# Global attention on 128 + 64 doubled channels with paired pieces, and a patch stage that takes over the first statistics

## The chip, the cores and the metric

One core of a Trainium2 chip runs the whole program in one launch. The metric is the device time of that launch in microseconds (us). In the profile PE is the matrix engine's matmul side and PEld its weight loads, DVE the vector engine, ACT the scalar engine, POOL the GpSimd engine, SP the engine whose queue issues most DMAs; a q behind a name (SPq) is an engine's sequencer.

## What is computed

The input is 16 pictures of 3 x 96 x 96 and a text of 16 x 512 tokens of 192 channels, all fp32. Cut to what matters here:

```
h = patch_tokens(x)                    # layer norm over a picture, 1x1 convolution, 36 patches -> 192 channels
h = concat([h, txt], axis=1)           # 16 x 548 x 192
h = h + linear_attention(norm(h))      # 12 heads, random features
h = h + gated_attention(norm(h))       # 3 experts of 64 channels, below
h = h + talking_heads(norm(h))
h = h + experts(norm(h))
# gated_attention(x), for each picture:
gate = softmax(relu(x @ Wg1 + bg1) @ Wg2 + bg2); keep the best two of three
q, k = split(x @ Wqk + bqk)
for e in 0, 1, 2:
    v_e = x @ Wv[e] + bv[e];  q_0 is convolved along the tokens
    y_e = softmax(causal(q_e k_e' / 8)) v_e * gate_e
out = concat(y) @ Wp + bp
```

## The kernel before

The 548 tokens of a picture lie in five tiles of up to 110 rows in the resident tensor X. The program is a row of phases, and all engines meet at a barrier between two of them: patch_tokens, performer (the linear attention), gated_attention (called the global attention in the change's name), then talking heads and experts. Every engine's order is written out by hand; semaphores tie the engines together.

**patch_tokens.** Pictures come in six groups of up to three. DVE first builds the product of the 1x1 convolution and the projection (weff, nine instructions, lines 398 and 400, after waiting for the projection's DMA), then takes the statistics of all pictures (lines 405 to 419, with a matmul and a power on POOL in between), then scales and shifts each group (428, 430). PE transposes and multiplies, DVE adds the position term (place, 273) and POOL issues the DMAs of the finished rows into X (375). The text of pictures 0 to 7 is fetched meanwhile.

**performer.** DVE starts with stats and aggregate (763, 768, 772) of the ten tiles of pictures 0 and 1, POOL raises to the power -1/2 (692), DVE normalizes (norm, 780), PE transposes (1009), ACT copies (920), PE makes the keys (1021). SP issues the text of pictures 8 to 15, then the weights of gated_attention (lines 661 to 676), then the first spill of a transposed picture (681).

**gated_attention.** Pictures go in eight pairs. A pair is one *round* of STEP = 15 steps, five query tiles t times three kinds (expert 0 and 1 of one picture each with both experts, expert 2 of both pictures); step s of a round has t = s // 3, and its scores have (t + 1) * 110 keys. In step n PE does, in this order: turn(n-2) for the first of two halves (1684), a piece, turn(n-2) for the second, a piece, the late turn of the last key tile (1690), the output product of every third step (produce, 1699 and 1700), the scores of step n+1 (1735), the values of step n-3 (1754). DVE does the causal mask (1499), two maxima (1503), a copy of the values (1512 to 1515), norm and statistics of the next pairs' tiles, the gates (gates_first in step 9, gates_last in step 10), its share of the pieces' copies, then 1/sum and the gate's weight (1535, 1538), and adds the output product to X (1545). ACT copies the turned probabilities (PT, 1599), raises to the exponential (1606), each twice, with its share of the pieces' copies after each. POOL multiplies the probabilities (1370), convolves (1314 to 1322, steps 6 to 8 and 11 to 13) and makes the next rstd (1299). The five last-tile scores use all four score banks, so the scores of the steps 12 to 15 wait for both exponentials of the step before.

Beside a round PE makes the next pair's *pieces*, in the order of PLAN: X (transposed normalized tokens, xT, 1648), Q, K, E (1639; 275 tokens each, 128 outputs; E is expert 2's q and k), H (hidden layer of the gate, 1657), L (its logits, 1669) and V (1674). A piece's result goes to one of two PSUM banks in turn (MISC, by the piece's number m; the late turn and the output product have numbers too). `begin(m)` waits until piece m-2 was taken from the same bank:

```
def begin(m):
    if m >= 2:
        pe.wait_ge(taken[m % 2], m // 2)
    return MISC[m % 2]
```

ACT takes X, H (four instructions, 1567), Q (1572), K (1576) and V (1581); DVE takes E (1419, 1420) and L (1429, 1431). The 192 channels are two chunks of 96 partitions; the second has a 97th row of ones, which brings the biases into the matmuls. The last round has no pieces; a few idle matmuls (spare, 1783 and 1784) stand in for them.

Of the kernel before, what the change touches and what calls it, by code (L numbers as in the profile page):

```python
# [20 lines left out]
B = 16  # L21
# [132 lines left out]
def early_weights(k, pf_ctx, ga_ctx):  # L154
# [7 lines left out]
    ga.wqk = sb(ga_ctx, "ga_wqk", [C + 1, KC, 2 * D])  # L162
    ga.wv = sb(ga_ctx, "ga_wv", [C + 1, KC, D])
    ga.wg1 = sb(ga_ctx, "ga_wg1", [C + 1, KC, HID])
# [10 lines left out]
    pf.eps = sb(pf_ctx, "pf_eps", [128, 1])  # L175

# [20 lines left out]
def text(k, eng, A, images, landed):  # L197
    b0, b1 = images[0], images[-1] + 1
    txt = A["txt"][b0:b1].rearrange("b n d -> n b d")
    for r0, r1 in ((NPATCH, NPATCH + 64), (NPATCH + 64, R)):  # L200
        eng.dma_start(k.X[r0:r1, b0 * T:b1 * T:T, :], txt[r0 - NPATCH:r1 - NPATCH]).then_inc(landed, 16)
    for t in range(1, T):
        n0 = t * R - NPATCH
        eng.dma_start(k.X[0:rows(t), b0 * T + t:b1 * T:T, :], txt[n0:n0 + rows(t)]).then_inc(landed, 16)


def patch_tokens(k, A):
# [5 lines left out]
    with ExitStack() as ctx:  # L213
# [37 lines left out]
        centred, scaled, normed = sem("centred"), sem("scaled"), sem("normed")  # L251
        turned, xT_in, prod, added, placed = sem("turned"), sem("xT_in"), sem("prod"), sem("added"), sem("placed")
# [8 lines left out]
        with nc.Block() as block:  # L261
# [80 lines left out]
            def _(pool):  # L342
# [29 lines left out]
                for b in range(B):  # L372
                    g, j = b // G3, b % G3
                    pool.wait_ge(added, g + 1)
                    pool.dma_start(X[0:NPATCH, b * T, :], y[j * NPATCH:(j + 1) * NPATCH, g, :]).then_inc(placed, 16)
                pool.wait_ge(placed, 16 * B)

            @block.vector
            def _(dve):
# [11 lines left out]
                dve.wait_ge(proj_in, 32)  # L391
                for c in range(CH):
                    for o in range(CH):
# [17 lines left out]
                dve.tensor_tensor(mv[:, :, 1], mv[:, :, 1], sq[:], ALU.add).then_inc(stats, 1)  # L411
                dve.wait_ge(averaged, 1)
# [13 lines left out]
                for g in range(NG3):  # L426
# [131 lines left out]
def performer(k, A):  # L558
# [13 lines left out]
    with ExitStack() as ctx:  # L572
# [3 lines left out]
        st = sb("st", [R, NT, 6])  # L576
        mv = sb("mv", [R, NT, 2])
        ve = sb("ve", [R, B, T])
        rstd = sb("rstd", [R, B, T])
# [29 lines left out]
        stat, aggr, var, powed, xn_in = (sem(n) for n in ("stat", "aggr", "var", "powed", "xn_in"))  # L609
# [7 lines left out]
        text_in, ga_in, warmed = (sem(n) for n in ("text_in", "ga_in", "warmed"))  # L617
        ga = k.ga
        NGA = 16 * (4 * 2 + 2 * E0 + 2 + 4 + 3 + 2)
# [23 lines left out]
        with nc.Block() as block:  # L643
            @block.sync
            def _(sp):
# [13 lines left out]
                text(k, sp, A, range(B // 2, B), text_in)  # L659
                for src, n, dst in ((0, 128, 0), (D, 128, 128), (128, 64, 256), (D + 128, 64, 320)):  # L660
                    sp.dma_start(ga.wqk[0:C, :, dst:dst + n], chunked(A["L0_ffn_Wqk"])[:, :, src:src + n]).then_inc(ga_in, 16)
                    sp.dma_start(ga.wqk[C:C + 1, KC - 1, dst:dst + n], row(A["L0_ffn_bqk"])[:, src:src + n]).then_inc(ga_in, 16)
                for e in range(E0):
                    sp.dma_start(ga.wv[0:C, :, e * HD0:(e + 1) * HD0], chunked(A["L0_ffn_Wv"][e])).then_inc(ga_in, 16)
                    sp.dma_start(ga.wv[C:C + 1, KC - 1, e * HD0:(e + 1) * HD0], row(A["L0_ffn_bv"][e])).then_inc(ga_in, 16)
                sp.dma_start(ga.wg1[0:C], chunked(A["L0_ffn_Wg1"])).then_inc(ga_in, 16)
                sp.dma_start(ga.wg1[C:C + 1, KC - 1, :], row(A["L0_ffn_bg1"])).then_inc(ga_in, 16)
# [20 lines left out]
            def _(pool):  # L688
                pool.memset(low[:], 3.0e38).then_inc(filled, 1)
                pool.wait_ge(filled, 1)  # L690
                pool.wait_ge(var, 1)
                pool.tensor_tensor(rstd[:, 0, :], ve[:, 0, :], k.mhalf[0:R, 0:T], ALU.pow).then_inc(powed, 1)
                pool.wait_ge(powed, 1)
                pool.memset(e[:, :, :, 2 * M:PW], 1.0).then_inc(filled, 1)
                pool.wait_ge(filled, 2)
                pool.memset(v1[:, :, :, W34:VW], 1.0).then_inc(filled, 1)
# [3 lines left out]
                for b in range(B + 2):  # L700
                    if b == 4:
                        pool.wait_ge(ga_in, NGA)
                        for c, s in ((C + 1, slice(128, 256)), (C + 1, slice(320, 384))):
                            pool.tensor_scalar(ga.wqk[0:c, KC - 1, s], ga.wqk[0:c, KC - 1, s], HD0 ** -0.5, None, ALU.mult)
                            pool.tensor_scalar(ga.wqk[0:C, 0, s], ga.wqk[0:C, 0, s], HD0 ** -0.5, None, ALU.mult)
# [52 lines left out]
            def _(dve):  # L758
# [43 lines left out]
                for u in range(T):  # L802
                    stats(u)
                for u in range(T):
                    aggregate(u)
                for u in range(T, 12):
                    stats(u)
                for u in range(T, 10):
                    aggregate(u)
                norm(0)  # L810
                norm(1)
                dve.wait_ge(filled, 4)
# [1997 lines left out]
```

## Time and profile before

| | |
|---|---|
| median of three runs | 4689.63 us (4688.78 to 4690.82) |
| the profiled execution, its own time | 4690.51 us |
| its span, first to last instruction | 4688.7 us |
| patch_tokens | 0 to 62.1 us |
| performer | 62.1 to 736.5 us |
| gated_attention | 736.5 to about 1303 us |
| talking heads and experts | to the end |

Times in rows count from the span's start. "A:B" rows sum a stretch; a timeline row merges neighbouring instructions of one kind and begins with its start and its length. An fp32 matmul of the program is two records of the profile, and matmul ends are modelled, so the distance from one start to the next is the safer reading. In brackets stands the idle time before an instruction and what ended it.

### The profile page before, as it was taken

The numbers are of one execution on the slowest core, as the hardware profiler recorded it, in microseconds if no ns is written. First come the engines' busy times: TensorE is split into PE (matmuls) and PEld (weight loads), VectorE is DVE, ScalarE is ACT, GpSimd is POOL, SyncE is SP. The second block draws the span as 40 slices with busy tenths as digits, with TensorE's granted clock in tenths as the row PEclk, the third lists the DMA queues.
The fourth block names the chain that finished last, engine by engine and source line by source line (L and its number), as shares of the span: only waits on it lengthen the run. The fifth ranks groups of instructions, "written<-read, shape, count | busy, mean of one in ns | idle before, by whom it ended". The sixth has DMA issues, their size and how long they took to land. (4 is left out here: it accounts for less than half of the span.)

```text
span 4688.7 us, 141401 instructions
## 1 busy us (share of the span) xinstructions
PE 4554.5 (97%) x58206; PEld 3744.1 (80%) x58206; DVE 2549.3 (54%) x7440; ACT 2183.1 (47%) x5035; POOL 1671.0 (36%) x2777
## 2 busy tenths in 40 slices
PE   6999998999889999999999999999999999999998
PEld 4666665776678888888888888888888888899998
DVE  5667886666555555455555555555555544442333
ACT  3443443555545554554455455445545544212443
POOL 1103335777633333333333333333333333001555
PEclk8999999999999999999999999999999999999999
DMA  4112110000000000000000000000000000232333
GB/s 109 23 30 48 38 31 7 1 2 1 1 14 2 13 13 2 20 13 13 3 13 13 2 13 13 7 8 13 13 2 13 13 3 17 74 90 66 65 65 56
DMA packets 122476, 110.77 MB, mean 24 GB/s; under 512 B 63975, under 2 KB 110396, under 8 KB 121844
## 3 DMA queue, kind: packets, MB, share of 16 engines
q1 hardware_dynamic: 94447, 66.34, 6.1%
q0 software_dynamic: 16768, 23.59, 2.9%
q10 hardware_dynamic: 10628, 11.80, 1.1%
q8 instruction: 472, 7.73, 0.7%
q14 instruction: 161, 1.31, 0.1%
HBM read 59.76 MB, written 41.48 MB: 22 GB/s over the span
## 5 line engine op out<-in xcount | busy, mean ns | idle before, releaser
L1937 POOL TENSOR_TENSOR th_qg<-th_qT,w_th_th 128x180 f32<-128x180 f32 x1760 | 846.3, 503 | 1617.1 <-PE PS L2231 1607.5
L2231 PE MATMUL PS<-th_kT,th_qg 64*125 64x274 f32 x10560 | 1420.5, 400 | 0.0
L2130 ACT ACTIVATE th_P<-PS 110x600 f32<-110x600 f32 x880 | 647.0, 735 | 1119.1 <-PE PS L2218 1119.1
L2048 DVE TENSOR_REDUCE th_nmx<-PS 125x1 f32<-125x548 f32 x880 | 641.0, 728 | 902.8 <-PE PS L2231 902.8
L2218 PEld LDWEIGHTS PS<-th_mixn,th_P 61*110 61x110 f32 x17600 | 985.8, 173 | 96.0 <-issue 20.2
L2231 PEld LDWEIGHTS PS<-th_kT,th_qg 64*125 64x125 f32 x10560 | 947.5, 184 | 136.9 <-issue 0.2
L2218 PE MATMUL PS<-th_mixn,th_P 61*110 61x60 f32 x17600 | 980.2, 254 | 3.5 <-ACT th_P L2130 1.8
L2140 ACT ACTIVATE th_P<-PS,th_nb 125x548 f32<-125x548 f32 x880 | 621.0, 706 | 106.9 <-DVE th_nb L2051 106.9
L1370 POOL TENSOR_SCALAR ga_P<-ga_P,ga_rw 110x110 f32<-110x110 f32 (+4 forms) x240 | 264.9, 1115 | 160.3 <-DVE ga_rw L1538 159.5
L2051 DVE TENSOR_SCALAR th_nb<-th_nmx,w_th_b 125x1 f32<-125x1 f32 x880 | 240.1, 273 | 32.2
L2256 PEld LDWEIGHTS PS<-th_P,th_v 110*32 110x32 f32 x11520 | 229.7, 110 | 28.6 <-issue 27.5
L2256 PE MATMUL PS<-th_P,th_v 110*32 110x90 f32 (+1 forms) x11520 | 250.2, 244 | 2.1 <-issue 1.2
L2065 DVE TENSOR_SCALAR th_mixn<-w_th_mix,th_rs 125x60 f32<-125x60 f32 x880 | 225.0, 256 | 31.8
L2455 POOL DMA_INDIRECT ex_cx<-ex_tokens,ex_token_of x77 | 77.0, 1000 | 343.1 <-DVE ex_b L2629 250.7
L1021 PE MATMUL PS<-w_pf_wK,pf_xT 64*110 64x456 f32 x960 | 196.1, 555 | 1.4 <-ACT pf_xT L920 1.4
L1599 ACT ACTIVATE ga_PT<-PS 110x440 f32<-110x440 f32 (+3 forms) x240 | 102.3, 426 | 199.2 <-PE PS L1684 196.8
L2387 ACT ACTIVATE ez_h<-PS,ex_cb 128x128 f32<-128x128 f32 x462 | 127.5, 375 | 133.3 <-PE PS L2715 133.3
L2468 POOL DMA_INDIRECT out_h<-ex_cy,ex_token_of x77 | 132.9, 1726 | 136.5 <-DMA out_h<-ex_cy,ex_token_of 120.5
L2400 ACT ACTIVATE ez_h<-PS,ex_bz 128x550 f32<-128x550 f32 x96 | 68.9, 719 | 241.2 <-PE PS L2654 241.2
L2140 ACT ACTIVATION_READ_ACCUMULATOR th_P<-PS,th_nb 125x1 f32 x880 | 178.1, 202 | 0.0
L2715 PE MATMUL PS<-ex_cxT,ex_wz 64*128 64x128 f32 x2772 | 175.5, 278 | 0.3 <-ACT ex_cxT L2418 0.3
L2715 PEld LDWEIGHTS PS<-ex_cxT,ex_wz 64*128 64x128 f32 x2772 | 160.7, 188 | 13.4 <-issue 12.8
(364 smaller groups left out, 6407.3 us busy)
## 6 DMA issues: line engine op xcount, KB each, us to landing
pf_xT<-pf_spill SPq DMA_DIRECT2D x32, 412.5 KB, 5.4
ex_tokens<-th_xn SPq DMA_DIRECT2D x124, 82.5 KB
pf_spill<-pf_xT SPq DMA_DIRECT2D x16, 412.5 KB, 3.7
ex_turned<-th_rT SPq DMA_DIRECT2D x16, 412.5 KB, 3.1
ex_x<-ex_turned SPq DMA_DIRECT2D x32, 206.2 KB, 4.4
out_h<-X SPq DMA_DIRECT2D x16, 330.0 KB
ex_w<-in_L_ffn_W ACTq DMA_DIRECT2D x18, 288.0 KB
ex_w<-in_L_ffn_W ACTq DMA_DIRECT2D x8, 576.0 KB
```

Of the source, the lines that this page charges most:

```text
L1021: ins = pe.matmul(PS[0:R, p + a, 0:HM + D], xT[half, slot(u), c, cols(u)], wK[half, c, :], start=c == 0, stop=c == NC - 1)
L1370: pool.tensor_scalar(P[:, n % 4, u, 0:keys(t)], P[:, n % 4, u, 0:keys(t)], rw[:, n % 4, u:u + 1], None, ALU.mult).then_inc(scaled, 1)
L1937: ins = pool.tensor_tensor(qg[:, m % SB, :, 64 * s:64 * s + HQ].rearrange("p c (h n) -> p c h n", n=QH), qT[:, im % 2, :, at + s * QH:at + ...
L2048: dve.tensor_reduce(nmx[:, p:p + 1], PS[0:MR, bank:bank + 2, 0:HK], AX.XY, ALU.max, negate=True) \
L2051: dve.tensor_scalar(nb[:, p:p + 1], nmx[:, p:p + 1], b1[:, 0:1], b1[:, 0:1], ALU.subtract, ALU.add) \
L2065: dve.tensor_scalar(mixn[:, p], mix[:], rs[:, p:p + 1], None, ALU.mult).then_inc(scaled, 1)
L2130: act.activation(P2[:, :, :, at * QT:(at + 1) * QT].rearrange("p t h (s n) -> p s (t h) n", s=2), PS[0:R, MB:MB + 2, 0:VO].rearrange("p s ...
L2140: act.activation(P[:, p, 0:N].rearrange("p (a n) -> p a n", a=2), PS[0:MR, bank:bank + 2, 0:HK], ACT.Exp, bias=nb[:, p:p + 1], accum_out=r ...
L2218: ins = pe.matmul(PS[0:R, MB + s, t * HQ:(t + 1) * HQ], P[a, p, t * R:(t + 1) * R], mixn[a, p], start=True, stop=True)
L2231: ins = pe.matmul(PS[0:MR, bank + a, 0:HK], qg[s, p, c, 0:MR], kT[s, im % 2, c, :], start=c == 0, stop=c == NC - 1)
L2256: ins = pe.matmul(PS[32 * j:32 * j + 32, bank, c * nq:(c + 1) * nq], v[:, b % 2, t].rearrange("p h d -> p (h d)")[:, at:at + 32], P2[:, t, ...
L2715: ins = pe.matmul(PS[:, 2 + 2 * (j % 2) + a, i * SL:(i + 1) * SL], cw[s, j % 2, c, i, :], cxT[s, j % 2, c, :], start=c == 0, stop=c == NC - 1)
```

## The change

- The tokens' 192 channels are 128 in one chunk and 64 in another, and these 64 are written twice, on partitions 0 to 63 and 64 to 127; so are their weights. norm has a second instruction for the copy.
- Q, K, E and V pieces are made in *groups* of two, in both banks: first both matmuls over 128 channels, then the two over 64 channels, each on its own half of the rows. `give` takes both banks first. PLAN is new.
- The biases leave the matmuls: ACT adds them when it copies H, Q and K, DVE when it copies E, and V moves from ACT to DVE as an addition.
- The weights come in 44 DMAs and not 25.
- In patch_tokens weff is built in three parts behind steps of the statistics, and the statistics of pictures 0 and 1 of performer are taken there (token_stats), with the first power on POOL.

```
+def token_stats(k, dve, tiles):
+    for u in tiles:
+        dve.bn_stats(pf.st[:, u, :], k.X[:, u, :]).then_inc(pf.stat, 1)
+    for u in tiles:
+        dve.wait_ge(pf.stat, u + 1)
+        dve.bn_aggr(pf.mv[:, u, :], pf.st[:, u, :]).then_inc(pf.aggr, 1)
...
+                    if b == B - 2:
+                        pool.wait_ge(pf.var, 1)
+                        pool.tensor_tensor(pf.rstd[:, 0, :], pf.ve[:, 0, :], k.mhalf[0:R, 0:T], ALU.pow).then_inc(pf.powed, 1)
...
                 dve.tensor_tensor(mv[:, :, 1], mv[:, :, 1], sq[:], ALU.add).then_inc(stats, 1)
+                weigh(0)
                 dve.wait_ge(averaged, 1)
...
+                weigh(1)
                 dve.wait_ge(powed, 1)
...
+                weigh(2)
                 dve.wait_ge(w_in, 16 * (2 + G3))
...
+                dve.wait_ge(text_in, 16 * (T + 1))
+                dve.wait_ge(placed_first, 16 * G3)
+                token_stats(k, dve, range(0, T))
                 place(dve, NG3 - 2)
+                token_stats(k, dve, range(T, 2 * T))
                 place(dve, NG3 - 1)
...
-        PLAN = ((("X", 0, 0),), (("X", 0, 1),), (("X", 0, 2),), (("X", 1, 0),), (("X", 1, 1), ("Q", 0, 0)),
-                (("X", 1, 2), ("Q", 0, 1)), (("H", 0, 0), ("K", 0, 0)), (("K", 0, 1),), (("L", 0, 0), ("E", 0, 0)),
-                (("E", 0, 1), ("Q", 1, 0)), (("Q", 1, 1), ("K", 1, 0)), (("K", 1, 1), ("E", 1, 0)), (("E", 1, 1), ("V", 0, 0)),
-                (("V", 0, 1), ("V", 0, 2)), (("V", 1, 0), ("V", 1, 1), ("V", 1, 2)))
+        PLAN = ((one("X", 0, 0),), (one("X", 0, 1),), (one("X", 0, 2),), (one("X", 1, 0), both("Q", 0)), (one("X", 1, 1),),
+                (one("X", 1, 2),), (one("H"), both("K", 0)), (both("Q", 1),), (one("L"), both("K", 1)), (both("E", 0),),
+                (both("E", 1),), (both("V", 0),), (both("V", 1),), ((("V", 0, 2), ("V", 1, 2)),), ())
...
+                        dve.tensor_scalar(xn[:, m % 4, D:2 * 128], X[:, b * T + t, 128:D], mv[:, b, t, 0:1],
+                                          rstd[:, p, b % 2, t:t + 1], ALU.subtract, ALU.mult).then_inc(xn_in, 1)
...
+                    if kind == "V":
+                        dve.wait_ge(given[m % 2], m // 2 + 1)
...
+                        dve.tensor_tensor(v[:, p % 2, i, 2 * j:2 * j + tiles, :],
+                                          PS[0:R, bank, 0:tiles * D].rearrange("p (t d) -> p t d", t=tiles),
+                                          bv[:].unsqueeze(1).broadcast_to([R, tiles, D]), ALU.add).then_inc(taken[m % 2], 1)
...
+                def give(n, group):
+                    kind, i, j = group[0]
                     p = n // STEP + 1
+                    ms = [number[n, piece] for piece in group]
+                    banks = [begin(m) for m in ms]
...
+                        w = slice("QKE".index(kind) * 128, ("QKE".index(kind) + 1) * 128)
+                        for g in range(2):
+                            pe.matmul(PS[:, banks[g], 0:HALF], wqk[:, 0, w], xT[:, i, 0, g * HALF:(g + 1) * HALF], start=True, stop=False)
+                        for g in range(2):
+                            half = slice(g * PC, (g + 1) * PC)
+                            pe.matmul(PS[:, banks[g], 0:HALF], wqk[half, 1, w], xT[half, i, 1, g * HALF:(g + 1) * HALF],
+                                      start=False, stop=True).then_inc(given[ms[g] % 2], 1)
```

## Rows read from the trace of the kernel before

**Rows 1.** Busy time of two phases: stretch, length, each engine's busy us (instructions), PEclk, DMA.

```profile
0.00:62.08 62.08, 29.68 (x154) 26.73 (x154) 31.41 (x65) 16.07 (x21) 12.59 (x37) 0.82 0.55 124
736.47:1303.00 566.53, 531.79 (x4168) 381.99 (x4168) 360.77 (x1256) 301.70 (x952) 389.59 (x346) 0.99 0.01 3
```

**Rows 2.** One steady round, mask to mask: steps 0-8, 9, 10, 11-14 (PE, PEld, DVE, ACT, POOL).

```profile
970.65:1003.53 32.88, 31.17 (x267) 21.33 (x265) 23.07 (x87) 19.66 (x71) 19.32 (x21) 1.00 0.01 1
1003.53:1009.28 5.75, 5.40 (x38) 3.63 (x37) 5.35 (x19) 2.88 (x8) 5.70 (x5) 1.00 0.01 3
1009.28:1014.36 5.08, 4.66 (x32) 3.10 (x32) 4.11 (x17) 2.35 (x8) 3.04 (x3) 1.00 0.00 0
1014.36:1037.21 22.85, 22.54 (x191) 18.06 (x188) 12.58 (x38) 12.52 (x32) 19.93 (x14) 1.00 0.01 1
sum 66.56, PE 63.77 PEld 46.12 DVE 45.11 ACT 37.42 POOL 47.99; mean PE 15.94 PEld 11.53 DVE 11.28 ACT 9.35 POOL 12.00
```

**Rows 3.** Steps 0 to 13 of a round with pieces, and of the last without.

```profile
970.65:1030.38 59.73, 56.95 (x452) 40.09 (x452) 42.35 (x151) 33.40 (x109) 42.05 (x38) 1.00 0.01 2
1235.78:1291.69 55.91, 46.27 (x394) 32.73 (x396) 28.73 (x95) 26.36 (x86) 30.17 (x29) 1.00 0.01 1
```

**Rows 4.** Timeline of PE: a K piece, four V tiles' matmuls, a pair of scores.

```profile
886.90 1.11 PE L1639 MATMUL PS<-ga_xT,w_ga_wqk 96*128 96x275 f32 x4
887.85 0.54 PE L1684 MATMUL PS<-ident,ga_P 110*110 110x110 f32 x4
...
892.23 1.47 PE L1674 MATMUL PS<-w_ga_wv,ga_xT 96*110 96x192 f32 x8
893.54 0.54 PE L1684 MATMUL PS<-ident,ga_P 110*110 110x110 f32 x4
...
935.48 0.62 PE L1735 MATMUL PS<-ga_k,ga_qc 64*110 64x440 f32 x1
935.93 0.53 PE L1735 MATMUL PS<-ga_k,ga_qc 64*110 64x440 f32 x1
```

**Rows 5.** Timeline of PEld in performer: loads for two 64-row matmuls.

```profile
153.59 0.18 PEld L1021 LDWEIGHTS PS<-w_pf_wK,pf_xT 64*110 64x110 f32 x2 [0.20 <-issue]
153.98 0.18 PEld L1021 LDWEIGHTS PS<-w_pf_wK,pf_xT 64*110 64x110 f32 x2 [0.20 <-issue]
```

**Rows 6.** Timeline of ACT: H taken in step 6, a PT copy in step 12.

```profile
993.00 1.60 ACT L1567 ACTIVATE ga_g<-PS 32x275 f32<-32x275 f32 x4 [0.16 <-PE PS L1657]
...
1021.55 0.54 ACT L1599 ACTIVATE ga_PT<-PS 110x440 f32<-110x440 f32 x1
```

**Rows 7.** Timeline of DVE: step 10's gates, the output's addition, E's second copy.

```profile
1012.82 0.19 DVE L1470 TENSOR_TENSOR ga_g<-ga_ge,ga_kept 110x30 f32<-110x30 f32 x1 [0.69 <-ACT ga_ge L1614]
...
1013.89 0.55 DVE L1545 TENSOR_TENSOR X<-PS,X 110x384 f32<-110x384 f32 x1
...
1074.63 0.45 DVE L1420 COPY ga_k<-PS 64x273 f32<-64x273 f32 x1
```

**Rows 8.** Timeline of POOL: first scaling of step 11, and the power of step 13.

```profile
1018.84 2.74 POOL L1370 TENSOR_SCALAR ga_P<-ga_P,ga_rw 110x440 f32<-110x440 f32 x2 [2.03 <-DVE ga_rw L1538]
...
1034.34 1.97 POOL L1299 TENSOR_TENSOR ga_rstd<-ga_ve,mhalf 110x10 f32<-110x10 f32 x1
```

**Rows 9.** Timeline of DVE in patch_tokens and at performer's start.

```profile
18.28 0.42 DVE L398 TENSOR_SCALAR tk_weff<-tk_projT,tk_cw 128x384 f32<-128x384 f32 x1 [12.42 <-DMA tk_projT<-in_tok_proj_wT]
...
23.56 5.62 DVE L405 BATCH_NORM_STATS2 tk_st<-tk_img 108x6 f32<-108x384 f32 x12
...
62.12 1.40 DVE L763 BATCH_NORM_STATS2 pf_st<-X 110x6 f32<-110x192 f32 x5 [4.37 <-PEq L2747]
...
66.35 1.59 DVE L780 TENSOR_SCALAR pf_xn<-X,pf_mv,pf_rstd 110x384 f32<-110x384 f32 x2
```

**Rows 10.** Timeline of SP: the first spill behind the weights; ACT: picture 3's copies.

```profile
87.27 27.19 SPq L681 DMA_DIRECT2D pf_spill<-pf_xT  x3
...
113.53 0.79 ACT L920 ACTIVATE pf_xT<-PS 128x330 f32<-128x330 f32 x2
```

More of the change, by code:

```diff
@@ L1210, in scores, with both, one, groups @@
             return flat[0:R, at:at + keys(t)]
-        PLAN = ((("X", 0, 0),), (("X", 0, 1),), (("X", 0, 2),), (("X", 1, 0),), (("X", 1, 1), ("Q", 0, 0)),
[3 rows of a table removed]
+        def both(kind, i):
+            return (kind, i, 0), (kind, i, 1)
+        def one(kind, i=0, j=0):
+            return ((kind, i, j),)
+        PLAN = ((one("X", 0, 0),), (one("X", 0, 1),), (one("X", 0, 2),), (one("X", 1, 0), both("Q", 0)), (one("X", 1, 1),),
+                (one("X", 1, 2),), (one("H"), both("K", 0)), (both("Q", 1),), (one("L"), both("K", 1)), (both("E", 0),),
+                (both("E", 1),), (both("V", 0),), (both("V", 1),), ((("V", 0, 2), ("V", 1, 2)),), ())
         TURN, GIVE, TAKE, OUT = 2, 3, 4, 5
+        def groups(n):
+            return PLAN[n % STEP] if n // STEP + 1 < PAIRS else ()
         def pieces(n):
-            return PLAN[n % STEP] if n // STEP + 1 < PAIRS else ()
+            return tuple(piece for group in groups(n) for piece in group)
         def late(n):
@@ L1627, in begin @@
                     return MISC[m % 2]
-                def give(n, piece):
-                    kind, i, j = piece
+                def give(n, group):
+                    kind, i, j = group[0]
                     p = n // STEP + 1
-                    m = number[n, piece]
-                    bank = begin(m)
-                    at = slice(j * HALF, (j + 1) * HALF)
-                    tiles = range(2 * j, min(2 * j + 2, T))
-                    def half(wc, rows_out):
-                        for c in range(KC):
-                            ins = pe.matmul(PS[0:rows_out, bank, 0:HALF], wc(c), xT[0:kin(c), i, c, at], start=c == 0, stop=c == KC - 1)
-                        return ins
+                    ms = [number[n, piece] for piece in group]
+                    banks = [begin(m) for m in ms]
+                    bank = banks[0]
@@ L1676, in give @@
-                    ins.then_inc(given[m % 2], 1)
+                            for c in range(2):
+                                x0 = ((t - 2 * j) * 2 + c) * R
+                                ins = pe.transpose(PS[:, bank, x0:x0 + R], xn[:, q % 4, c * 128:(c + 1) * 128], ident[0:R, 0:R])
+                        ins.then_inc(given[ms[0] % 2], 1)
+                        return
+                    for ii in range(2) if kind == "H" or j == 2 else (i,):
+                        for jj in range(3):
+                            wait_taken(pe, (p, ("X", ii, jj)))
@@ L1763, in _ @@
                 for n in range(FIRST, END):
-                    ps = pieces(n)
+                    gs = groups(n)
                     for u in range(2):
@@ L1771, in _ @@
                             stream(1)
-                        if u < len(ps):
-                            give(n, ps[u])
-                    for piece in ps[2:]:
-                        give(n, piece)
+                        if u < len(gs):
+                            give(n, gs[u])
                     if late(n):
```

202 lines of the change are left out of this document (108 added, 94 removed).

## The prediction

> **What bounds the kernel now.** I read first the busy time by phase. The changed matmuls are all in gated_attention, 566.5 us long, with PE busy for 531.8 of them; the patch phase is 62.1 us long and keeps no engine busy for much over half of that [rows 1]. Next the windows of one steady round, cut at the mask of each step. A round takes 66.56 us and PE is busy for 63.77: by this view alone PE is the bound. But the reader is to see two windows beside it: in step 9 DVE is busy for 5.35 of 5.75 us, and in steps 11 to 14 POOL for 19.93 of 22.85 [rows 2]. Then the comparison that tells what PE work is worth. The last round makes no pieces: PE has 10.7 us less to do in fourteen steps, DVE 13.6 less, and these steps take 55.91 us instead of 59.73 [rows 3]. So even without any piece a round gains only 3.8 us; behind PE stands a chain score, mask, exponential, turn, PT copy, next score that is almost as long. Whether the change wins depends on what its waits do to that chain, more than on PE's sum.
>
> **What PE saves.** A Q, K or E piece occupies PE for 887.85 - 886.90 = 0.95 us: four records of 275 columns, 0.2375 each. Eight V records of 192 columns take 893.54 - 892.23 = 1.31, or 0.164 each [rows 4]. Two 64-row matmuls that run together take the time of one: in performer 0.39 us from one pair of records with 456 columns to the next [rows 5], in the scores 0.45 with 440 columns, where full-rate columns would take 0.38 [rows 4]. The score pair enters and leaves row halves, the performer's pair stays in them; I book 0.09 us a record pair, between 0 and 0.09. A group of Q, K or E is then 4 x 0.2375 + 2 x (0.2375 + 0.09) = 1.60 instead of 1.90, a V group of four tiles 1.31 + 4 x 0.164 + 0.18 = 2.14 instead of 2.62, the group of two last tiles 1.16 instead of 1.31. Six groups save 1.8, the V groups 1.1: 2.9 us a round, up to 4.4 if switching is free. The X transposes have as many records as before and stay as they are.
>
> The Trainium skill, "TensorEngine Tiling (Array Packing)", section Theoretical Speedup, gives up to 2x where a dimension is at most 64; by that the saving would be the 4.4 us. The same page, Key Properties, says that changing the tiling mode drains the engine, and there the score pair's extra 0.09 agrees; by it the saving is the 2.9.
>
> **What waits.** A group takes both banks at its start, so it waits until the piece right before it was taken, where before PE wrote one bank while the other was emptied. And PLAN moves work forward: until step 8 there were five Q, K or E pieces (4.75 us), now four groups (6.4): +1.6. I go through a round.
>
> Steps 0 to 8: the group of Q behind X waits for ACT's copy of X, 0.5. The group of K in step 6 waits for all four copies of H, 1.60 us on ACT [rows 6], of which the turn between covers 0.24: +1.4. In step 7 the output product waits for the first Q copy, +0.3; in step 8 K waits for DVE to take L, +0.5. PE idles 1.7 us in these steps now [rows 2], and the shorter steps 4 and 5 give back about 1.3 of such waits. Sum +1.6 + 0.5 + 1.4 + 0.3 + 0.5 - 1.3 = +3.0. DVE's second norm instruction (64 of 192 columns, 0.2 us, two a step) disappears in DVE's waits except in step 0.
>
> Step 9: DVE takes two E pieces, not one, after gates_first. One is two copies of 0.45 [rows 7], so +0.9, of which 0.4 us was idle [rows 2]: +0.5.
>
> Step 10: this is the worst place. Both E pieces are taken by DVE behind gates_last, which itself waits for ACT's exponential of step 10 [rows 7]. The output product of the same step needs the bank of the first, and the scores of step 11 are queued behind it on PE. From the mask at 1009.28 the gates' wait ends at 1012.82, the gates at +4.3, the first E at +5.2, the output product (eight records of 192 columns, 1.31) at +6.5, the next mask after 0.9 of scores and hand-over, +7.5 less 0.2 because ACT has nothing to take before: 7.3 instead of 5.08, +2.2.
>
> Steps 11 and 12: the whole V group of 2.14 stands between the two turns, where a piece of 0.95 stood. The second PT copy and the second exponential queue behind the second turn (0.54 [rows 6] and 0.9 with the hand-over), and the scores of a last tile wait for that exponential: +1.2 each, +2.4. That V is on DVE as 0.55 [rows 7] adds nothing there, DVE is idle for 10.3 us of these four steps [rows 2].
>
> Steps 13 and 14: PE has 1.16 and nothing instead of four V groups' worth, yet little comes back. POOL works without a gap from the scaling at 1018.84 to the end of the power at 1036.31 [rows 8], DVE's norm of step 14 waits for that power, and the next mask is behind it on DVE. I give back 0.4 and add 0.4 for the norm's second instructions: 0.
>
> The sum is 3.0 + 0.5 + 2.2 + 2.4 = +8.1 us a round. Seven rounds carry pieces: +57. Lower bound of a round: none of the new waits shows, and it gains what taking all pieces away gains, -3.8 [rows 3]. Upper bound: no wait is given back, +1.3, and the gates' step costs 1 us more: +10.5. Before round 0 the pieces stand alone; there PE and the copies alternate, the V groups save 1.5, E waits for its copies: -2, between -5 and +5.
>
> **The patch stage.** DVE waits 12.42 us for the projection, builds weff until 23.56 and only then starts the statistics [rows 9]. The pictures' DMAs were issued at the very start; they have landed by 23.56, since nothing waits there, and I take 16.5, between 13 and 18 (1.7 MB at the phase's rate of 124 GB/s and some more [rows 1]). Statistics at 16.5: -7.1. weff's three parts are 1.7 us each; two fill the waits for the mean and the power (+1.0 and +0.3 beyond them), the third comes whole before the next work, +1.7: -4.0 in all, between -1 and -6. Behind it token_stats costs DVE 2 x 2.0 us, mostly while PE multiplies, and POOL's power stands ahead of the last DMA: +0.8. In performer the statistics go, from 62.12 to the norm at 66.35: -4.2, and -0.3 as that norm runs alone [rows 9]. Sum -8, between -3 and -11. The removed ones-row memset and the smaller memset of v1 lie beside other work: 0.
>
> Nineteen DMAs more on SP, 0.3 to 0.6 us each, push the first spill from 87.27 to 93 - 99; its buffer is overwritten by picture 3's copies at 113.53 [rows 10]. Hidden; were it not, each us late would be a us.
>
> **Sum.** 4690.5 (the profiled run's own time, 0.9 above the median) + 57 - 2 - 8 = 4737.5; against the median 4737.
>
> **The rivals.**
> 1. The waits overlap. PE is one step ahead of DVE at many places, and a late piece may be caught up before its reader. Then a round costs +2 to +4: 4690 + 21 - 10 = 4701, up to 4715. For it: PE's idle 1.7 us in steps 0 to 8 [rows 2]. Against: the chain of step 10 has no slack, since DVE itself is the late one.
> 2. Faster: PE is the bound as its busy share says, and the copies keep up with the groups. Place: the bank waits in steps 6, 8 and 10; from the point where they sum to less than PE's 2.9 us the round shortens. Seven rounds by -2.9 and -10: 4660, at the bound of -3.8 4653. Against: H's 1.60 on ACT and gates_last ahead of E on DVE stand in the program's order.
> 3. The array packing does nothing: halves run one after the other. Against: the performer's pairs run together [rows 5]. A round costs another 3 to 4 us: 4760.
> 4. No change: gain and waits cancel (a round +1): 4687 to 4698.
>
> The Trainium skill, same page, section PSUM Bottleneck, says that tiling speeds up the multiplication and not the emptying of PSUM; and Gotcha 1 says that two row tiles can't use one bank at once. That is the rule by which a group must take both banks, as forecast. No row here shows two halves in one bank.
>
> **How the numbers follow.** Forecast (a round +5 to +10, 4716 to 4757) 0.57; rival 1 0.16; rival 4 0.08; rival 2 0.11; rival 3 or longer 0.08. The range 4699 to 4762 holds the forecast, rival 1 and most of rival 3. About 0.2% (9 us) is what a measurement tells from no change: faster by more 0.12, within 0.09, slower 0.79. The forecast's own range is 4716 to 4757.
>
> **What would show it.** In the profile after: rounds of 71 to 76 us between step-0 masks; step 10 at 7.3 us with the output product released by DVE's E copy; PE waiting about 1.4 us behind H in step 6; steps 11 and 12 about 1.2 longer with the scores released by the exponential; performer's first matmul near 60 us and not 68; the spill still ahead of its reader. It would be wrong if step 10 stays near 5 us, or if the group's wait in step 6 is hidden.

## The result, and the profile after

The changed kernel takes 4828.43 us in the median of four runs (4813.28 to 4831.44), against 4689.73 for the kernel before on the same chip: a ratio of 1.029, 95% interval 1.027 to 1.031. It is slower, as forecast, but by 139 us and not by 47; the time lies outside the range of 4699 to 4762. The profiled execution is the fastest of the four, 4813.28 us with a span of 4811.5, so I first account for its 122.8 us of span, and then for the 15 to 18 us between it and the others.

Windows of the changed kernel: the patch phase, gated_attention whole, and its start up to the first mask [rows 1].

```profile
0.00:58.86 58.86, 29.38 (x154) 26.23 (x154) 34.77 (x87) 16.06 (x21) 13.92 (x38) 0.88 0.59 131
...
731.09:1425.80 694.71, 571.45 (x4150) 383.25 (x4152) 409.04 (x1382) 295.37 (x904) 387.60 (x345) 0.90 0.01 2
...
731.09:787.14 56.05, 40.85 (x158) 24.42 (x158) 23.52 (x98) 8.51 (x20) 21.08 (x29) 0.70 0.06 12
```

Gated_attention starts 5.4 us earlier (731.09, before 736.47) and is 128 us longer [rows 1]. PE is busy for 40 us more, although it has less to multiply, and the column behind the engines, TensorE's granted clock, is 0.90 where it was 0.99. The seven rounds with pieces, from the first mask to that of the last round, went from 459.3 to 571.0 us (787.14 to 1358.15), so +111.7; the stretch ahead of them from 40.0 to 56.05, +16.0; the rest is +0.4.

Windows of one steady round of the changed kernel: steps 0 to 8, 9, 10, 11, 12 to 14 [rows 2].

```profile
1195.09:1235.54 40.45, 36.92 (x269) 24.97 (x270) 24.88 (x92) 22.19 (x74) 22.27 (x23) 0.87 0.01 1
1235.54:1242.05 6.51, 5.33 (x43) 3.21 (x44) 6.03 (x21) 2.79 (x9) 2.67 (x3) 1.00 0.00 1
1242.05:1251.97 9.92, 6.62 (x25) 3.81 (x25) 6.39 (x21) 1.89 (x6) 5.49 (x4) 0.73 0.00 0
1251.97:1258.99 7.02, 5.79 (x46) 4.28 (x48) 3.41 (x10) 2.29 (x6) 0.85 (x1) 0.90 0.01 2
1258.99:1278.41 19.42, 15.46 (x145) 11.41 (x146) 10.96 (x30) 8.19 (x20) 16.65 (x12) 0.97 0.00 1
sum 83.32, PE 70.11 PEld 47.68 DVE 51.66 ACT 37.34 POOL 47.94; mean PE 14.02 PEld 9.54 DVE 10.33 ACT 7.47 POOL 9.59
```

This is what the prediction did not have: a clock column below 1.00 in four of the five windows, where before it is 1.00 in all four. PE now idles for 13.2 us of a round (83.32 - 70.11); it idled for 2.8. Step 10 shows how the two hang together. First the output product and the scores of step 10 in the kernel before, then the timeline of PE and of DVE in step 10 of the changed kernel, whose mask is at 1242.05 [rows 7]:

```profile
1011.42 0.58 PE L1699 MATMUL PS<-w_ga_wpa,ga_c 128*110 128x192 f32 x2 [0.42 <-ACT ga_q L1572]
...
1012.91 0.99 PE L1735 MATMUL PS<-ga_k,ga_q 64*110 64x440 f32 x4
1013.84 0.79 PE L1754 MATMUL PS<-ga_PT,ga_v 110*64 110x110 f32 x12
```

```profile
1243.49 0.49 PE L1742 MATMUL PS<-ident,ga_P 110*110 110x110 f32 x3
1247.29 0.98 PE L1757 MATMUL PS<-w_ga_wpa,ga_c 128*110 128x192 f32 x2 [3.30 <-DVE ga_k L1462]
...
1250.12 1.81 PE L1793 MATMUL PS<-ga_k,ga_q 64*110 64x440 f32 x4
1251.86 0.45 PE L1812 MATMUL PS<-ga_PT,ga_v 110*64 110x110 f32 x2
```

```profile
1245.30 0.19 DVE L1521 TENSOR_TENSOR ga_g<-ga_ge,ga_kept 110x30 f32<-110x30 f32 x1 [0.39 <-ACT ga_ge L1661]
...
1246.21 0.50 DVE L1460 TENSOR_SCALAR ga_q<-PS,w_ga_bqk 64x275 f32<-64x275 f32 x1
1246.73 0.51 DVE L1462 TENSOR_SCALAR ga_k<-PS,w_ga_bqk 64x275 f32<-64x275 f32 x1
```

The gates' wait ends 3.25 us behind the mask (forecast 3.54) and the first E copy 5.2 (forecast 5.2). Up to here the forecast holds. But PE sat still for 3.3 us, and the output product then takes 2.83 us (1247.29 to 1250.12) where it took 1.49 before (1011.42 to 1012.91; the forecast had 1.31), and the scores 1.74 instead of 0.93. The granted clock of this step is 0.73: it stood at half in part of it. Step 10 takes 9.92 us, not 7.3.

PE's waits in the same round of the changed kernel: total us, times, the longest.

```profile
PE PS L1793 <- ACT ga_P L1653: 3.8, 3, 1.3
PE PS L1757 <- DVE ga_k L1462: 3.3, 1, 3.3
PE PS L1730 <- issue: 3.2, 3, 1.8
PE PS L1742 <- ACT ga_PT L1646: 1.3, 3, 0.7
```

The first three were forecast: scores behind the second exponential, the output product behind E, the groups behind H, L and E (a group waits for two banks, which the view puts down to "issue"; in this round 1.80 behind H, 0.22 behind L and 1.18 behind E). The turns' wait for a PT copy is not new, the kernel before has 1.3 us of it in a round too.

### The profile page after: what moved, and what is told of

It reads as the page before. It is cut to its first block and busy times, and to the rows that moved or that the text cites. A ratio compares the mean times of both kernels' runs of the same rounds, so it can differ in the third digit from the quotient of the medians.

```text
span 4811.5 us, 141359 instructions
## 1 busy us (share of the span) xinstructions
PE 4597.0 (96%) x58206; PEld 3747.3 (78%) x58206; DVE 2597.7 (54%) x7568; ACT 2176.7 (45%) x4987; POOL 1663.7 (35%) x2776
```

## The experiments

All times are medians; the kernel before had 4689 to 4691 us beside each. My theory from the trace of the changed kernel was A: the groups' waits are the cause, and the clock doubles their price. The rival B: what the layout brought (copies with a bias, V on DVE, the second norm instruction, the 64-row matmuls) costs the time even without groups. In the expectations C says that idle time costs once as a wait and once as the half clock behind it, W that the waits alone cost; the others are told where they stand.

**The front alone.** The kernel before with token_stats, weigh() and performer's shorter start; gated_attention and its loads as before.

> Only the front of the change: the pictures' statistics ahead of weff's parts, token_stats in the patch stage, the smaller memset; gated_attention, its weights and its loads are the kernel before's. In the trace of the changed kernel gated_attention starts 5.4 us earlier than before, although 19 more loads were issued. Theory A (the front is a gain of its own that the rounds then lose many times over): 4682 to 4685. Rival: the gain ahead of performer is given back at the border to gated_attention: 4689 to 4691.

4683.24 (4680.76 to 4685.16, ten runs), ratio 0.998, interval 0.9972 to 0.9991: a small gain and the only version here that is faster than the kernel before. Windows of the kernel before, of about 200 and 272 of PE's matmuls in performer, and of the same matmuls in the front-only kernel, followed by its start of gated_attention:

```profile
376.80:401.80 25.00, 19.64 (x202) 11.61 (x202) 16.30 (x33) 8.72 (x17) 11.36 (x33) 1.00 0.16 36
706.30:736.47 30.17, 22.31 (x272) 15.18 (x272) 22.93 (x49) 8.39 (x13) 7.57 (x19) 0.94 0.00 1
```

```profile
367.00:394.10 27.10, 21.43 (x203) 12.50 (x202) 16.36 (x33) 8.73 (x17) 11.49 (x33) 0.94 0.15 32
698.40:731.47 33.07, 26.96 (x272) 18.79 (x272) 23.10 (x49) 8.46 (x14) 7.59 (x19) 0.76 0.01 1
731.47:768.52 37.05, 34.12 (x157) 24.28 (x158) 18.64 (x81) 10.36 (x26) 23.07 (x30) 0.89 0.09 18
```

Performer's first matmul starts at 58.57 instead of 68.02, 9.5 us earlier, and up to 367 the same matmuls stay 9.8 us ahead: the edit gains more than the forecast's 8. Then the clock falls to half at two other places than before, and these two windows give back 2.1 and 2.9 us; gated_attention starts 5.0 us earlier. There the clock happens to be better (0.89 instead of 0.83) and 3.0 come back: the first mask is at 768.52 instead of 776.48, 8.0 earlier. Waits of which nothing was changed have moved against the clock. The -8 of the forecast comes out at the first mask, but by three errors that cancel (+1.8, -4.8, +3.0): that is luck.

**Pieces one at a time.** The changed kernel with the order of before and groups of one.

```
-                (one("X", 1, 2),), (one("H"), both("K", 0)), (both("Q", 1),), ...
+                (one("X", 1, 2), one("Q", 0, 1)), (one("H"), one("K", 0, 0)), (one("K", 0, 1),), ...
```

> The changed kernel with the pieces made one at a time by the order of the kernel before; layout 128 + 64, biases in the copies, V on DVE and the two norm instructions stay as changed. Theory A (the groups' waits for two banks and what follows from them are the whole loss; PE's sum is then that of before, 0.95 us a piece): 4680 to 4695. Theory B (the new copies, V on DVE, the second norm instruction or the second matmul on 64 rows cost the time by themselves): above 4750. Halfway means both.

4797.95. Theory A was half wrong: without any group 115 of the 145 us over the front-only kernel are still there (in the profiled executions the seven rounds sum to 557.7 us, against 459.8 in the front-only kernel and 571.0 in the changed one). Three things show in its trace. First, a piece: the timeline of PE in the version with V on ACT (below), at the full clock; the same rows stand in both.

```profile
1201.69 0.65 PE L1729 MATMUL PS<-ga_xT,w_ga_wqk 128*128 128x275 f32 x2
1202.26 0.73 PE L1732 MATMUL PS<-ga_xT,w_ga_wqk 64*128 64x275 f32 x2
1202.92 0.59 PE L1741 MATMUL PS<-ident,ga_P 110*110 110x110 f32 x4
```

A piece alone takes 1.23 us (1201.69 to 1202.92) against 0.95 [rows 4]: going into the row half and out again costs 0.28, and nothing runs beside it. My theory had 0.95. The Trainium skill, "TensorEngine Tiling (Array Packing)", Key Properties, says that changing the tiling mode drains the engine; this row agrees. Second, PE waits for DVE in step 14:

```profile
1267.64 0.90 PE L1724 MATMUL PS<-w_ga_wv,ga_xT 64*110 64x192 f32 x4
1270.74 0.58 PE L1718 MATMUL PS<-w_ga_wv,ga_xT 128*110 128x192 f32 x2 [2.21 <-DVE ga_v L1470]
```

Third, in step 9, which DVE bounds, one comparison of 110 x 10 elements takes 1.41 us. The same line has 0.174 in the kernel before. DVE, then POOL in that kernel:

```profile
1233.02 0.19 DVE L1505 TENSOR_TENSOR ga_gd<-ga_g,ga_gm 110x30 f32<-110x30 f32 x1
1233.24 1.41 DVE L1506 TENSOR_TENSOR ga_kept<-ga_g,ga_m 110x10 f32<-110x10 f32 x1
```

```profile
1233.29 1.33 POOL L1364 TENSOR_TENSOR ga_qc<-ga_qc,ga_side 64x548 f32<-64x548 f32 x1
```

It ends 0.03 us behind POOL's addition, which fits a wait for it. Its line has a median of 1.41 us over the eight rounds.

**V back on ACT**, V's bias left out of the computation, with single pieces, and with the groups.

> The kernel with single pieces (4798), V taken by ACT as before instead of DVE; V's bias is left out of the computation. Step 14 took 9.6 to 10.5 us there instead of 6.8, with PE waiting 2.6 us for DVE's add of V, which stands behind the norm and so behind POOL's power. Theory D (V on DVE is what the layout costs in step 14, and through the clock in steps 0 and 1): steps 14, 0 and 1 go back to 14.1 us from about 19.8, 4750 to 4762. Rival (the norm's second instruction and the wider X copies are late there): above 4785.

> The changed kernel with V taken by ACT, V's bias left out of the computation. My prediction's step (V on DVE adds nothing, DVE is idle for 10.3 us of these four steps): 4824 to 4832. Theory D, from the single pieces, where V on ACT gave back 52 us: at least half of that here, 4776 to 4802.

With single pieces 4745.91: 52 us less, theory D holds. Step 14 goes from 9.6 - 10.2 us to 6.73. With the groups 4827.85, no change: there my prediction's step stands, V on DVE adds nothing, because the groups put V into steps 11 to 13, away from the norm. So the 115 us of the single version are not all in the changed kernel; the two have different diseases. The single version also gives the cleanest sight of the clock. Two of its rounds, with the same instructions:

```profile
1153.67:1225.16 71.49, 67.72 (x520) 44.37 (x518) 50.16 (x169) 39.34 (x119) 48.00 (x41) 1.00 0.01 1
936.03:1010.69 74.66, 70.94 (x520) 46.18 (x518) 50.35 (x168) 39.46 (x119) 48.00 (x41) 0.95 0.01 1
```

71.49 at the full clock, 74.66 where step 10 fell into the half clock. And at the full clock PE has 67.7 us of work where it had 63.8 [rows 2]: twelve pieces of Q, K and E at 0.28 more are 3.4 of these 3.9 us.

**The second norm instruction** left out as well; the doubled channels are zero.

> Single pieces with V on ACT (4746, rounds of 71.49 us at the full clock against 66.59 with the old layout), and the norm's second instruction left out too, so that the doubled channels are zero. Theory N (DVE's second instruction, 0.31 us, two a step, costs the 0.9 in step 0 and shifts the compare in step 9 under POOL's addition, where it took 1.41 us instead of 0.17): a round 0.9 to 2.5 shorter, 4728 to 4740. Rival (X copies on 128 partitions and the H copies with a bias): 4744 to 4747.

4748.16: no gain. Its full-clock rounds take 71.3 us, 0.2 less, and the comparison in step 9 still takes 1.41. Theory N falls: the instruction is hidden, as forecast, and the meeting with POOL comes from elsewhere.

**Matmuls that nobody reads, to keep PE busy while it waits.** The first try wrote them to VB in steps 6, 10, 11, 12 and 14, the second to the free score banks in step 10, the third is the second with the right number:

```
+                            pe.wait_ge(exped, 2 * n)
+                            for _ in range(count):
+                                pe.matmul(PS[:, 2 * ((n + 1) % 2), 0:2 * D], ident[0:C, :], wqk[0:C, 0, :], start=True, stop=True)
```

> The changed kernel with matmuls of 384 columns that nobody reads where PE waits: 5 ahead of K in step 6, 3 ahead of E in step 10, 9 ahead of the output product of step 10, 3 each ahead of the scores in steps 11, 12 and 14. No other work is changed and no wait is shortened. Theory A1 (the granted clock falls to half after these waits, for 20.4 of the 83.3 us of a steady round, and the work then takes twice its time): a round 6 to 9 us shorter, 4765 to 4785. Rival A2 (the waits alone are the price, the clock only goes along): 4828, or some us more for the fillers that outlast their wait.

> The changed kernel with 12 matmuls of 384 columns that nobody reads in step 10 alone, 3 ahead of the E group and 9 ahead of the output product, written to the score banks of the next step, which are free by a wait that the scores of the next step have anyway. PE idled 1.3 and 3.3 us at these places. Theory C (the idle time costs once as a wait and once more as the half clock behind it: output product 2.83 us instead of 1.49, scores 1.74 instead of 0.92): step 10 falls from 9.9 to about 7.7 us, a round by 2.2, 4828 to 4805 to 4815. Theory W (waits only, the half clock would be there anyway or costs nothing): no change, or some us more.

> As the run with twelve such matmuls in step 10, with as many as fit the idle time: one took 0.645 us there (two records), not 0.33, so nine outlasted their wait by 2.4 us. Here 1 ahead of the E group and 5 ahead of the output product. Theory C: the output product then takes 1.4 us and the scores 0.93 at the full clock; step 10 takes 8.1 to 8.3 us instead of 9.92, and 4828 becomes 4812 to 4818, less if the clock falls elsewhere instead. Theory W: 4828 or above.

4854.7, 4832.64, 4800.2. The first two were badly built: one filler takes 0.645 us, not the 0.33 that I had used, so they outlasted the waits, and those of the first waited ahead of step 10's group for DVE's copy of VB (the bank of the values), which held up the turn, ACT's exponential and the gates (step 10: 17.0 us). Only the third tests the theory. Windows of its steps 10 and 11:

```profile
1227.87:1235.64 7.77, 7.71 (x33) 4.38 (x32) 6.52 (x22) 1.89 (x6) 3.64 (x3) 1.00 0.01 2
1235.64:1242.02 6.38, 5.14 (x46) 3.76 (x44) 3.42 (x10) 2.29 (x6) 2.55 (x3) 1.00 0.00 0
```

Its output product and scores, timeline of PE:

```profile
1233.28 0.58 PE L1757 MATMUL PS<-w_ga_wpa,ga_c 128*110 128x192 f32 x2
...
1234.77 0.99 PE L1793 MATMUL PS<-ga_k,ga_q 64*110 64x440 f32 x4
```

Step 10 takes 7.77 instead of 9.92 us, step 11 6.38 instead of 7.02, with six matmuls more to do: 2.8 us a round, 20 of the 28 in seven rounds (the profiled seven rounds sum to 552.3 us, 18.7 less). The output product is back at 1.49 us (1233.28 to 1234.77). No wait was taken away; only what PE did in it changed. (The other 8 lie where the half clock falls in the rest, the last round above all: two of the four runs have 4791 and 4793, two 4808 and 4812; the profiled one, 4812, has 77.71 us in the last round.)

> The kernel with single pieces (4798), with 5 such matmuls ahead of Q in step 10 (PE idle 2.0 us there) and 7 ahead of the last V piece of step 14 (PE idle 2.6 us there). After both places its trace shows the half clock for 6.8 to 10.2 us, and step 10 takes 8.3 to 9.0 instead of 5.08, step 0 5.3 to 5.5 instead of 3.03. Theory C: steps 10, 11, 0 and 1 give back about 2.2 + 1 + 2.2 + 1 us a round, 4750 to 4765. Theory W: 4798 or above.

4777.86, 20 us less instead of 33 to 48. Every steady round is at the full clock and step 10 takes 6.17 instead of 8.3 - 9.0, but seven fillers in step 14 were again too many (11.2 us instead of about 9.9).

> The changed kernel, with such matmuls in PE's waits ahead of round 0 alone (1 to 3 ahead of each group of Q, H, K, L, E and V, 17 in all, in VB, which nothing reads yet). The stretch from the phase's start to the first mask took 56.0 us instead of 40.0, with the clock at half for most of 748 to 779, and a group of Q, K or E 3.4 us instead of 1.7. Theory C: 5 groups at 1.7 us less: 46 to 49 us for the stretch, 4818 to 4821. Theory W (the copies set the pace, PE's speed doesn't matter there): 54 us or more, 4826 or above.

4818.1. The stretch ahead of the first mask:

```profile
729.40:777.62 48.22, 43.18 (x190) 24.40 (x190) 24.99 (x99) 8.50 (x20) 21.10 (x29) 0.93 0.07 14
```

48.2 us instead of 56.05, at a granted clock of 0.93 instead of 0.70. Half of the +16 was the clock.

**The order on DVE.** E ahead of gates_last in step 10; then E ahead of the gates in steps 9 and 10; then the same in the front-only kernel.

```
+                    for piece in pieces(n):
+                        take(n, piece)
                     if s == 10:
                         gates_last(p + 1)
-                    for piece in pieces(n):
-                        take(n, piece)
```

> The changed kernel, DVE takes the two E pieces of step 10 ahead of gates_last instead of behind it. E was given at 1243.49 and taken from 1246.21 in the trace. Theory A: the output product comes 2.7 us earlier, 19 us in seven rounds; with the half clock that follows this wait gone too, up to 5.2 a round: 4792 to 4809. Rival (the gates, later by the two copies, hold the scaling and so the turns up): 4825 or above.

> The changed kernel with the same swap in steps 9 and 10. With step 10 alone it took 4784. Theory S: E0 leaves its banks 1.6 us earlier, so E1 is given and the turn behind it comes earlier, a round 1 to 2 us less: 4770 to 4778. Rival: step 9 is DVE's own chain, 4782 to 4788.

> The front of the change alone (4683), with DVE taking the piece of step 9 ahead of gates_first and that of step 10 ahead of gates_last. PE idles 0.5 us in step 10 for the bank of the E piece of step 9. Theory S (the bank comes free 1.6 us earlier): 0.5 us a round less, 4677 to 4681. Rival (DVE itself is the chain in step 9, busy 5.35 of 5.75 us, so its order changes nothing, and the second exponential comes later): 4683 to 4688.

The first gives 4784.28, 44 us less: the best single edit to the changed kernel, at the step that I had named the worst. It was expected to give 19 to 36, and the rounds give 32 of that (539.3 us in the profiled seven, against 571.0); the rest of the 44 is the last round, which takes 61.04 us here and probably some 77 in most runs of the changed kernel (below). One of its rounds has the full clock up to the end of step 14. Its steps 0 to 8, 9, 10, 11, 12 to 14:

```profile
1095.42:1132.58 37.16, 32.14 (x266) 21.38 (x268) 24.81 (x92) 21.59 (x73) 22.32 (x23) 1.00 0.01 2
1132.58:1139.10 6.52, 5.33 (x43) 3.21 (x44) 6.04 (x21) 2.80 (x9) 2.69 (x3) 1.00 0.00 0
1139.10:1145.83 6.73, 5.46 (x39) 3.43 (x37) 6.26 (x21) 1.89 (x6) 3.16 (x3) 1.00 0.00 1
1145.83:1151.42 5.59, 4.35 (x33) 2.95 (x32) 3.41 (x11) 2.40 (x6) 3.19 (x3) 1.00 0.00 0
1151.42:1170.87 19.45, 15.46 (x145) 11.42 (x146) 10.98 (x31) 8.20 (x20) 16.68 (x12) 0.98 0.01 1
sum 75.45, PE 62.74 PEld 42.39 DVE 51.49 ACT 36.89 POOL 48.05; mean PE 12.55 PEld 8.48 DVE 10.30 ACT 7.38 POOL 9.61
```

75.45 us, still 8.9 above 66.56. The second swap loses instead of gaining: 4802.83, and 4698.35 in the front-only kernel (ratio 1.0016, interval 1.0007 to 1.0025; its rival was right, and by more than it said). The rounds carry it: 556.8 us in seven, 17.5 more than with the first swap. In the front-only kernel step 9 grew from 5.76 to 6.39 us, and again POOL's timeline tells why. DVE, then POOL:

```profile
1074.62 1.21 DVE L1473 TENSOR_TENSOR ga_gd<-ga_g,ga_gm 110x30 f32<-110x30 f32 x1
```

```profile
1074.45 1.33 POOL L1342 TENSOR_TENSOR ga_qc<-ga_qc,ga_side 64x548 f32<-64x548 f32 x1
```

The swap pushed a 0.19 us subtraction under POOL's addition, and it took 1.21. From the second round on steps 10 and 11 together then take 11.3 to 12.9 us instead of 9.7, with the half clock in step 10.

**K0 ahead of H**, in step 4, so that it doesn't wait for H's copies.

> The changed kernel with the group of K0 in step 4 behind X instead of in step 6 behind H. PE waited 1.8 us for the copies of H in step 6, and the half clock followed for 3.4 us. My prediction's step (K behind H costs 1.4 a round): step 6 falls from 6.9 to 4.9 us and step 4 grows by about 1: a round 1 to 2.5 shorter, 4810 to 4822. Rival: step 4 pays all of it: 4826 to 4832.

4845.52, 17 us more: a miss. Step 6 fell to 4.96 us as expected and step 7 from 6.1 to 4.4, but step 4 rose from 3.2 to 6.5, step 9 by 1.1, step 10 by 1.6. In step 9 the gates' first product, 0.19 us elsewhere, took 1.30, under the same addition of POOL.

**The last round, and all together.**

> The changed kernel with one unread matmul of 384 columns in each of the first four steps of the last round. Theory L (its timed runs, 4828, entered the last round at the half clock and stayed there, 77 us instead of 57; its profiled run, 4813, didn't): all runs at 4811 to 4818. Rival (the 15 us lie elsewhere): 4826 to 4832.

> The swap in steps 9 and 10, the unread matmuls ahead of round 0 and in the last round, two more ahead of K in step 6 and one ahead of the scores in steps 11, 12 and 14: the changed kernel as near the full clock as fillers that fit its waits bring it. Theory C (half of the loss is the clock, half the waits and switches, which stay): half clock for under 60 us of the phase, 4735 to 4755, still above 4690. Rival 1 (the clock was nearly all): 4690 or below. Rival 2 (the fillers only trade waits): above 4765.

> The swap in step 10 alone (4784), with the unread matmuls ahead of round 0, in the first four steps of the last round, two ahead of K in step 6 and one ahead of the scores in steps 12 and 14. Theory C: rounds of 75.5 to 76.5 us, as the one of that kernel without a half clock, and 8 us less ahead of round 0: 4755 to 4766, so at the full clock the change would still be 70 us slower. Rival (the clock is all that is left): below 4730. Rival (fillers only trade waits): 4775 or above.

4813.59 (4812.88 to 4819.16), 4774.19 and 4764.59. The first bears on the 15 to 18 us between the profiled run of the changed kernel and its others, of which no trace was kept. Windows of the last round, of the changed kernel, of the one with fillers ahead of round 0, and of the one with groups and V on ACT:

```profile
1358.15:1415.67 57.52, 47.88 (x394) 33.74 (x396) 28.74 (x94) 26.35 (x86) 30.98 (x29) 0.97 0.01 1
```

```profile
1347.92:1422.84 74.92, 65.29 (x394) 45.71 (x396) 29.20 (x95) 26.32 (x86) 30.73 (x29) 0.69 0.00 1
```

```profile
1358.35:1436.03 77.68, 68.05 (x394) 47.22 (x396) 29.20 (x95) 26.31 (x86) 30.72 (x29) 0.65 0.00 1
```

The same 394 records take 57.5 or 77.7 us, and the seven rounds ahead of them sum to 571.0 and 571.1 us in the first and the third kernel: the 20 us between their profiled runs (4813 and 4833) are the last round. Where the clock falls to half at its border, within 2 us to either side, it stays there for 54.6 us in the third kernel and for 47.8 in the second. With the four unread matmuls the round takes 62.95 us at 0.92, so they keep about three quarters of it away. The last run brings theory C's 4755 to 4766: three of its seven rounds take 75.44 to 75.47 us, at a granted clock of 0.98 to 1.00. With most of the clock restored and with the best order found the change is still 74 us slower than before: 62.6 of that are the seven rounds and 8.4 the last, which takes 64.31 us at 0.89. The second run, both swaps with fillers, lies on the side of its rival 2; the half clock still fell in step 10 of every round.

## Why the prediction was right or wrong

The direction was right, and so were the new waits of the rounds and the steps in which they stand; the size was a third, because the forecast had no term for the clock and almost none for the stretch ahead of round 0. One round, by step; the third column is put together from the rows of the full-clock round (steps 0 to 9 and 12 to 14, whose order the swap leaves as it is) and of the third filler run (10 and 11):

| steps | before | forecast | at the full clock | measured |
|---|---|---|---|---|
| 0 to 8 | 32.88 | +3.0 | 37.16, +4.3 | 40.45, +7.6 |
| 9 | 5.75 | +0.5 | 6.52, +0.8 | 6.51, +0.8 |
| 10 | 5.08 | +2.2 | 7.77, +2.7 | 9.92, +4.8 |
| 11 | 4.64 | +1.2 | 6.38, +1.7 | 7.02, +2.4 |
| 12 to 14 | 18.21 | +1.2 | 19.45, +1.2 | 19.42, +1.2 |
| sum | 66.56 | +8.1 | 77.28, +10.7 | 83.32, +16.8 |

Timeline of PE in the third filler run: one group at the full clock, which ends at 1223.97.

```profile
1222.27 1.11 PE L1730 MATMUL PS<-ga_xT,w_ga_wqk 128*128 128x275 f32 x4
1223.31 0.73 PE L1733 MATMUL PS<-ga_xT,w_ga_wqk 64*128 64x275 f32 x4
```

1. **The sum of the seven rounds, +57, is the step that failed.** It measured +111.7. At the full clock it is 7 x 10.7 = 75 by the round of the table, and the other 37 are put down to the clock. That split is an estimate: the same round as measured would give 7 x 16.76 = 117 and not 111.7, since the first and the last of the seven are shorter, so it is good to some 6 us. The prediction charged each wait once. In this kernel an idle PE pays twice: about 3.3 us of waiting in step 10 cost another 2.15 in the work behind it, which came back when the wait was filled.
2. **PE saves 2.9 a round**: over-sized. At the full clock PE's sum went from 63.77 to 62.74, by 1.0. A group of Q, K or E takes 1.70 to 1.76 us, not 1.60, a V group 2.24, not 2.14. I had charged 0.09 for each pair of records in the half; a single piece shows 0.28 for one visit. "Up to 4.4 if switching is free" was never near.
3. **Steps 0 to 8, +3.0**: +4.3 in waits and work. K waits behind H for 1.8 us (forecast 1.4); moved ahead of H it cost more, in step 4.
4. **Step 9, +0.5, and steps 12 to 14, +1.2**: right. V on DVE costs nothing with the groups, and the second norm instruction 0.2 us a round (tried with single pieces).
5. **Step 10, +2.2**: the chain was right to 0.3 us up to E's copy; 2.15 of the rest are the clock. Of the 0.5 that remain at the full clock 0.18 is the output product, which the forecast had at 1.31 and which took 1.49 in the kernel before already; the others were not tried apart. E's copies take 0.50 instead of 0.45 each and the group 1.76 instead of 1.60.
6. **Before round 0, -2 (between -5 and +5)**: +16.0. This term failed too, by 18. About 8 is the clock, by the fillers. The rest are put down to waits, read from the trace and not tried apart: a group starts only when both banks of the one before are emptied, so PE and the copies take turns, where before one bank was written while the other was emptied. That -2 counted E's wait but not the same wait ahead of every other group.
7. **The patch stage, -8** (between -3 and -11): the edit gains 9.8, against 8 forecast, and the clock takes up to 4.8 of it before gated_attention; 5.0 and, in the changed kernel, 5.4 arrive there. That the 19 loads more are hidden holds.
8. **The last round, no term**: +1.6 in the profiled execution (57.52 against 55.91 us). The other runs are 15 to 18 us longer; that it is the last round at the half clock is shown in the version with V on ACT and argued for this one.
9. **Rival 3 (packing does nothing)**: refuted: the four 64-row records of a group take 0.66 us together, and two take 0.66 alone. Rivals 1, 2 and 4 are refuted by the full-clock round.

What stays open: which wait in particular sets off the half clock at the start of a round (it moved when others were filled), why it then lasts as long as it does, and the rest of PE's saving.

## What to carry to other kernels

Cost a new wait of a nearly full TensorE twice: once as idle time, and once as the work behind it at the lower level of the clock (1.2 GHz), and read the granted clock beside every stretch, before and after. Doubling up 64-row matmuls saved PE 0.2 us on two pieces here (1.70 against 1.90), because each visit to the half between 128-row matmuls costs 0.28 us; it should save more where many of them follow each other, which no run tried. And a group that must hold two banks gives up the overlap of writing and emptying. And where DVE is the chain, look at what POOL does at that moment before moving its instructions by a microsecond.

## What the hardware showed beyond that

- The half clock can hold through a stretch that is far from idle: in the last round PE is busy for 68.05 of 77.68 us at a mean granted clock of 0.65, in another run for 47.88 of 57.52 at 0.97, with the same records. What decides it is not shown. The clock fell to half within 2 us of the round's start in nine of the changed kernel's versions and stayed there for 6.8 us (with four unread matmuls at the start), 13.7 (two versions, one of them with such matmuls), 41.0 (two), 47.8, 54.6 (two) and 58.0; in the profiled run of the changed kernel itself it did not fall there. The Trainium skill, "TensorE: Matmul & The Clock Gate", section "HAM oscillation — how this bites in real kernels", describes a kernel whose waits throw the clock back again and again; the rounds here agree. That a busy PE stays at half through most of a round, these runs show beyond it.
- Shifting the same matmuls by 9.8 us moved the places at which the clock falls: 5 us lost and 3 won in a kernel whose work was otherwise the same. A comparison of two versions that differ by less than this needs the granted clock beside it.
- DVE's small instructions with two SBUF operands (0.16 to 0.19 us) took 1.21, 1.30 and 1.41 us in three kernels, each time until POOL's tensor_tensor of 1.33 us was done. The kernel before has such meetings too: eight instructions that begin under that addition take 0.62 to 1.17 us, and all end 0.02 to 0.05 us behind it. The Trainium skill, "SBUF — State Buffer", section Who interferes with whom, says that a DVE instruction with two SBUF inputs contends with a GpSimd instruction that reads SBUF, and that the later one waits whole; this agrees. (In the 1.41 us case DVE's record begins 0.05 us ahead of POOL's, which is within what POOL's spans are good for.) Under POOL's tensor_scalar, which reads SBUF too, the page's rule does not hold as it stands: in the kernel before 69 of 86 such instructions that begin under it took 0.16 to 0.20 us, and the 17 longer ones (0.27 to 0.66) ended while POOL's went on for another 0.5 to 0.9 us. Here the measurement decides.
